# A contiguous table of the earlier vectors, and two constant matmuls per step, in a 64-matrix Householder tridiagonalisation

## What is computed

```
deg = jnp.sum(A, axis=-1)
Lap = deg[..., :, None] * jnp.eye(n, dtype=A.dtype) - A
Lap_norm = d_isqrt[..., :, None] * Lap * d_isqrt[..., None, :]
_, U = jnp.linalg.eigh(Lap_norm)
agg = jnp.einsum('bmn,bmd->bnd', U, features)
```

## Time and profile before

| | |
|---|---|
| median of 3 runs | 5151.7 us |
| lowest, highest | 5149.34, 5155.43 us |
| the profiled execution | 5160.19 us |
| its span, first to last instruction | 5157.9 us |
| mean granted TensorE clock over the span | 0.686 of 2.4 GHz |

### The profile page before, as it was taken

How to read it: one execution, slowest core, us unless ns; L and a number is a source line. 1 busy time by engine, 2 the same in 40 slices (tenths; PEclk the granted TensorE clock), 3 DMA queues, 4 the chain that set the end, 5 groups by cost and what they waited for, 6 DMA issues and landing times.

```text
span 5157.9 us, 57427 instructions
## 1 busy us (share of the span) xinstructions
PE 2378.0 (46%) x15702; PEld 1593.0 (31%) x15702; DVE 4163.5 (81%) x18604; ACT 1313.2 (25%) x4350; POOL 122.0 (2%) x53
## 2 busy tenths in 40 slices
PE   0555555555526717519349063344105821020399
PEld 0222222233324314215124063243105820020266
DVE  4788878888779999999999888686996979989522
ACT  0000000011113233242342233122442412224154
POOL 0000000000000000000000010010003100000000
PEclk9766666665556857758668576676557965555699
DMA  6000000000110000000000112005000030020120
GB/s 144 14 15 25 25 16 19 19 22 25 30 31 9 9 9 17 0 9 17 9 1 0 17 31 45 0 9 124 0 0 9 17 124 0 0 114 0 49 66 17
DMA packets 142060, 140.50 MB, mean 27 GB/s; under 512 B 28445, under 2 KB 128426, under 8 KB 134826
## 3 DMA queue, kind: packets, MB, share of 16 engines
q1 hardware_dynamic: 141738, 136.97, 9.8%
HBM read 110.43 MB, written 26.41 MB: 27 GB/s over the span
## 4 chain that ended last, share of the span: by engine, by line
DVE 60%; PE 27%; DMA 5%; issue 4%; ACT 3%; SPq 1%; DVEq 0%; ACTq 0%; PEldq 0%
PE psum L2038 7%; PE psum L1678 5%; DVE big_a L381 2%; DVE gvec L385 2%; DVE big_b L1107 2%; PE psum L2062 2%; DMA big_b<-rows_dram 1%; DVE vt L529 1%; PE psum L2240 1%; DVE big_b L716 1%; DMA vt<-pairs_dram 1%; DVE sc_t L951 1%; DVE big_b L707 1%; DVE big_b L711 1%; DVE big_a L953 1%
## 5 line engine op out<-in xcount | busy, mean ns | idle before, releaser
L2038 PE MATMUL psum<-big_a 128*32 128x508 f32 (+59 forms) x4032 | 443.7, 606 | 54.1 <-issue 50.9
L1627 PE MATMUL psum<-plane,big_a 128*128 128x128 f32 x192 | 50.2, 430 | 608.8 <-ACT big_a L1543 587.2
L2013 PE MATMUL psum<-plane,big_b 128*128 128x128 f32 x126 | 54.6, 433 | 442.7 <-DVE big_b L396 442.1
L2038 PEld LDWEIGHTS psum<-big_a 128*32 128x32 f32 x4032 | 174.3, 157 | 255.0 <-issue 175.5
L1678 PE MATMUL psum<-big_b 128*128 128x512 f32 x544 | 245.5, 613 | 0.0
L2234 PE MATMUL psum<-plane,big_b 128*128 128x128 f32 x192 | 37.7, 378 | 443.2 <-DVEq L1308 426.7
L2224 PE MATMUL psum<-big_b 128*128 128x128 f32 x384 | 71.7, 372 | 349.7 <-ACT big_b L2138 349.7
L1627 PEld LDWEIGHTS psum<-plane,big_a 128*128 128x128 f32 x192 | 36.0, 220 | 622.6 <-ACT big_a L1543 599.6
L1837 DVE TENSOR_REDUCE f_ln<-psum 128x4 f32<-128x512 f32 x32 | 22.1, 689 | 233.6 <-PE psum L1952 157.8
L1996 ACT COPY big_a<-psum 128x64 f32<-128x64 f32 x109 | 29.1, 267 | 662.7 <-PE psum L2047 662.7
L2219 PE MATMUL psum<-vt,big_b 128*128 128x128 f32 (+1 forms) x384 | 72.3, 375 | 261.1 <-ACT big_b L1330 261.1
(11 more groups left out here) (729 smaller groups left out, 9270.4 us busy)
## 6 DMA issues: line engine op xcount, KB each, us to landing
big_a<-rows_dram SPq DMA_DIRECT2D x4, 4096.0 KB, 13.9
vt<-pairs_dram SPq DMA_DIRECT2D x504, 32.0 KB
big_a<-rows_dram SPq DMA_DIRECT2D x4, 2048.0 KB, 17.3
pairs_dram<-big_a SPq DMA_DIRECT2D x252, 32.0 KB, 1.8
big_a<-rows_dram SPq DMA_DIRECT2D x2, 3072.0 KB, 15.6
big_b<-rows_dram SPq DMA_DIRECT2D x2, 3072.0 KB, 22.5
big_b<-adj SPq DMA_DIRECT2D x2, 2048.0 KB, 17.6
big_b<-adjT SPq DMA_DIRECT2D x2, 2048.0 KB, 39.5
```

The costliest lines, as they stand in the source:

```text
L1627: ins = t.transpose(psum[0:parts, bank, g * N:(g + 1) * N], src(g), ident)
L2013: t.transpose(psum[:, 1, 0:SLOTS], x_rows[0:SLOTS, k % 2, :], whole).then_inc(S("x_node_ps"), 1)
L2038: ins = t.matmul(psum[i * SPAN:i * SPAN + MW, 0, 0:4 * wide], v_masked[:, i, q * MW:(q + 1) * MW], anode[:, g:g + 4, k + 1:N + 2 * u], sta ...
```

## The change

**The table.** `ring` goes. The pairs now lie in `past` (P), an array of 128 x 16 in `big_a`: for one element the values of all the panel's vectors are contiguous, 64 bytes from element to element. Lines 317 and 381 then walk over the vectors first and over the elements second, reading P and writing T in runs of 2u contiguous values.

**Its upkeep.** v and w are still written as contiguous rows, because TensorE and the DMAs read them: v to `v_rows` (8 rows in `big_b`), w to `w_rows` (4 rows of its own, a tile that the kernel before had allocated and not used). Two `tensor_copy` on VectorE per step put them into P as well: the w row in `reflect`, behind the norm of x and before the square root is asked for (u > 0, 109 times), and v in `advance`, between the sum of line 385 and the dot product of line 389 (all but the last step of a panel, 109 times). The stores of w must now have landed four steps back, where before a slot of the ring was reused after eight.

**The constant matmuls.** After the transposition of v, in steps with k < 64, u > 0 and not the last of the panel, TensorE does two fp32 matmuls of the identity with 512 columns of `plane`, a constant. They write PSUM bank 7, which nothing reads before the panel's update overwrites it. These are 45 steps and 90 matmuls.

```diff
-        ring = carve(PAIRS // 2, 2, N)
+        past = carve(N, PAIRS)
-        x_rows = big_b[:, 0:2 * N].rearrange("p (k n) -> p k n", n=N)
+        VR = 8
+        v_rows = big_b[:, 0:VR * N].rearrange("p (k n) -> p k n", n=N)
+        x_rows = big_b[:, VR * N:(VR + 2) * N].rearrange("p (k n) -> p k n", n=N)
...
                 n_x = lp.go(v.tensor_tensor_reduce(junk[:, x], raw[:, x], raw[:, x], 1.0, 0.0, ALU.mult, ALU.add, s2x))
-                if k >= FULL:
-                    v.wait_ge(S("v_stored"), 16 * (stored_before(k) + 1))
+                if j:
+                    v.wait_ge(S("w_row"), k)
+                    n_w = lp.go(v.tensor_copy(P[:, k + 1:, many - 1], w_rows[0:SLOTS, (k - 1) % 4, k + 1:]))
+                if k >= VR:
+                    v.wait_ge(S("v_stored"), 16 * (k - VR + 1))
...
                 if j:
-                    pairs = pairs_of(k, u)
-                    partners = ring_h[:, place(k - u):place(k - u) + u, ::-1, k + 1]
-                    v.wait_ge(S("w_row"), k)
-                    lp.go(v.tensor_tensor(by_pair(T[:, live, 0:many]), pairs, over(partners, w, 3), ALU.mult))
-                    n_b = lp.n
+                    partners = P[:, k + 1, 0:many].rearrange("p (j t) -> p j t", t=2)[:, :, ::-1]
+                    lp.after(n_w)
+                    n_b = lp.go(v.tensor_tensor(by_pair(T[:, live, 0:many]), by_pair(P[:, live, 0:many]), over(partners, w, 1), ALU.mult))
...
-                    weights = coef[:, 0:many].rearrange("p (j t) -> p j t", t=2)
-                    lp.go(v.tensor_tensor(by_pair(T[:, live, 4:4 + many]), pairs_of(k, u), over(weights, w, 3), ALU.mult))
+                    lp.go(v.tensor_tensor(T[:, live, 4:4 + many], P[:, live, 0:many], over(coef[:, 0:many], w, 1), ALU.mult))
...
                 v.wait_ge(S("v_row"), k + 1)
+                if u < size - 1:
+                    lp.go(v.tensor_copy(P[:, k + 1:, many], vk))
...
-                if k >= FULL:
-                    v.wait_ge(S("w_stored"), 16 * (stored_before(k) + 1))
+                if k >= 4:
+                    v.wait_ge(S("w_stored"), (k - 3) * 16)
...
-            by_pair = lambda ap: ap.rearrange("p w (j t) -> p j t w", t=2)
-            pairs_of = lambda k, u: ring_h[:, place(k - u):place(k - u) + u, :, k + 1:]
+            by_pair = lambda ap: ap.rearrange("p w (j t) -> p w j t", t=2)
...
                     if u < size - 1:
                         t.wait_ge(S("v_row"), k + 1)
-                        t.transpose(psum[:, 6, 0:SLOTS], ring[0:SLOTS, place(k), 0, :], whole).then_inc(S("v_node_ps"), 1)
+                        t.transpose(psum[:, 6, 0:SLOTS], v_rows[0:SLOTS, k % VR, :], whole).then_inc(S("v_node_ps"), 1)
+                        if u and k < N // 2:
+                            for _ in range(2):
+                                t.matmul(psum[:, 7, :], whole, plane[:, 0:4, :], start=True, stop=True)
```

More of the change, by code:

```diff
@@ L142, in graph_net @@
         anode = carve(B, AW)
-        carve(AW)
-        ring = carve(PAIRS // 2, 2, N)
+        past = carve(N, PAIRS)
         terms = carve(N, 4 + PAIRS)
         PER = 16 // TILES
+        carve(AW)
         v_masked = carve(TILES, PER * (MW + 8))
@@ L274, in v_tridiagonal @@
             st(v.memset(tri_h[:, :, :], 0.0))
+            st(v.memset(w_rows[:, :, :], 0.0))
             st(v.memset(gs_h[:, 0:1], 1e-30))
@@ L283, in v_tridiagonal @@
             own = pl["own"][0:SLOTS, 0:4]
-            ring_h, T = ring[0:SLOTS], terms[0:SLOTS]
+            V = v_rows[0:SLOTS]
+            P, T = past[0:SLOTS], terms[0:SLOTS]
             d_, e_, tau_ = (tri_h[0:SLOTS, i, :] for i in range(3))
@@ L287, in v_tridiagonal @@
             v.wait_ge(leaves_stored, 32)
-            st(v.memset(ring[:, :, :, :], 0.0))
-            st(v.memset(big_b[:, 0:2 * N], 0.0))
+            st(v.memset(big_b[:, 0:(VR + 2) * N], 0.0))
             v.sem_inc(S("tri_started"), 1)
@@ L298, in reflect @@
                 be, tau = e_[:, k:k + 1], tau_[:, k:k + 1]
-                v_new = ring_h[:, place(k), 0, :]
+                v_new = V[:, k % VR, :]
                 v.wait_ge(S("x_row"), k + 1)
                 n_x = lp.go(v.tensor_tensor_reduce(junk[:, x], raw[:, x], raw[:, x], 1.0, 0.0, ALU.mult, ALU.add, s2x))
-                if k >= FULL:
-                    v.wait_ge(S("v_stored"), 16 * (stored_before(k) + 1))
-                if k == FULL + VR - 2:
+                if j:
[3 more added lines that the diff above has]
+                    v.wait_ge(S("v_stored"), 16 * (k - VR + 1))
+                if k == VR - 2:
                     v.wait_ge(S("lap_stored"), 48)
@@ L353, in reflect, with advance @@
                 return n_e
-            def advance(k, u, n_e):
+            def advance(k, u, size, n_e):
                 j, w, many = u, N - k - 1, 2 * u
@@ L359, in advance @@
                 tau = tau_[:, k:k + 1]
-                vk = ring_h[:, place(k), 0, live]
+                vk = V[:, k % VR, live]
                 if not j:
@@ L398, in advance @@
                 n_d = lp.go(v.tensor_tensor(d_[:, k + 1:k + 2], moved[:, k + 1:k + 2], c2, ALU.add))
-                if k >= FULL:
-                    v.wait_ge(S("w_stored"), 16 * (stored_before(k) + 1))
+                if k >= 4:
+                    v.wait_ge(S("w_stored"), (k - 3) * 16)
                 lp.after(n_s)
-                wn = ring_h[:, place(k), 1, live]
+                wn = w_rows[0:SLOTS, k % 4, live]
                 v.scalar_tensor_tensor(wn, vk, a2, scaled[:, live], ALU.mult, ALU.add).then_inc(S("w_row"), 1)
                 lp.after(n_d)
-            by_pair = lambda ap: ap.rearrange("p w (j t) -> p j t w", t=2)
-            pairs_of = lambda k, u: ring_h[:, place(k - u):place(k - u) + u, :, k + 1:]
+            by_pair = lambda ap: ap.rearrange("p w (j t) -> p w j t", t=2)
             def stale_of(k, u):
@@ L422, in v_tridiagonal @@
                         n_e = reflect(b0 + u, u)
-                    advance(b0 + u, u, n_e)
+                    advance(b0 + u, u, size, n_e)
                     lp.rewind()
@@ L2024, in t_tridiagonal @@
                         t.wait_ge(S("w_row"), k)
-                        t.transpose(psum[:, 5, 0:SLOTS], ring[0:SLOTS, place(k - 1), 1, :], whole).then_inc(S("w_node_ps"), 1)
+                        t.transpose(psum[:, 5, 0:SLOTS], w_rows[0:SLOTS, (k - 1) % 4, :], whole).then_inc(S("w_node_ps"), 1)
                     t.wait_ge(S("x_weights"), k + 1)
@@ L2304, in _ @@
             sy.wait_ge(S("tri_started"), 2)
-            sy.dma_start(pairs_dram[N - 2:, 0].rearrange("k g n -> g k n"), ring[0::2, VR - 2:, 0, :]).then_inc(S("lap_stored"), 16)
+            sy.dma_start(pairs_dram[N - 2:, 0].rearrange("k g n -> g k n"), v_rows[0::2, VR - 2:, :]).then_inc(S("lap_stored"), 16)
             def pair_rows(k, u, c):
@@ L2316, in _ @@
                     sy.wait_ge(S("v_row"), k + 1)
-                    sy.dma_start(pairs_dram[k, 0], ring[0::2, place(k), 0, :]).then_inc(S("v_stored"), 16)
+                    sy.dma_start(pairs_dram[k, 0], v_rows[0::2, k % VR, :]).then_inc(S("v_stored"), 16)
                     if u:
@@ L2320, in _ @@
                     sy.wait_ge(S("w_row"), k + 1)
-                    sy.dma_start(pairs_dram[k, 1], ring[0::2, place(k), 1, :]).then_inc(S("w_stored"), 16)
+                    sy.dma_start(pairs_dram[k, 1], w_rows[0::2, k % 4, :]).then_inc(S("w_stored"), 16)
                     if u == 0 and k_panel:
```

## The result

The changed kernel takes 5069.06 us in the median of 4 runs (5064.97 to 5076.41), the kernel before, beside it, 5150.62 (5149.34 to 5155.43). The ratio is 0.9842, 95% interval [0.9826, 0.9857]: 81.6 us less, where 76 less (5076 us) was predicted and 5040 to 5112 was the range.

A forecast was written before the change was run, and what follows sets the result against it. VectorE was taken to bound `advance` alone and, with TensorE's matvec, the way to line 369. The table's -53.7 us and the clock's -22 made -76 from 5151.7, so 5076 us; range 5040 to 5112.

The forecast's parts named there:

- What bounds: Tridiagonalisation step: up to line 369 the longer of VectorE's `reflect` and TensorE's matvec decides; after it, `advance` is VectorE alone.
- The products: Lines 317 and 381: contiguous runs take them from 2.07 to about 1.06 ns per element, saving 53.2 us each.
- The copies: 109 of w in `reflect`, 109 of v in `advance`: 14.2 us for w, 3.9 for v after free time.
- The second half: `advance`, line 369 to the next x row: -53.2 us from line 381, +3.9 for copying v, -49.3 in sum.
- The table alone: Both halves of the step without the constant matmuls: -49.3 us after line 369, -4.4 before it, -53.7 together.
- The clock: Constant matmuls shorten TensorE's idle time, so matvecs at u = 2 and 3, k < 64, run faster: -22 us.
- No help from the clock: Rival: the constant matmuls don't hold TensorE's clock, only the table's gain is left: 5098 us, chance 0.20.
- clock held everywhere: Rival: matvecs at u = 2 to 7, k < 64, all run at 2.4 GHz, -69.2 us: 5029 us, chance 0.12.
- Half rate: Rival: lines 317 and 381 gain only half, 1.55 ns per element: 5104 us, chance 0.08.
- slow rate: Rival: lines 317 and 381 keep their rate, the 218 added copies only cost, +23 us: 5175 us, chance 0.05.
- Cover: Constant matmuls hide behind `advance` at no cost (bound +5 us); no wait for w stores; panel ends keep their length.

The follow-up runs named there:

- the sized matmuls: Changed kernel with constant matmuls sized to end 0.3 us before the next x row, in all steps with u > 0 except a panel's last: 0.9689 against the kernel before.

## Why the prediction was right, point by point

**What bounds.** Right. The two halves of a step behave as described: what VectorE saves in `advance` shortens the step, what it saves in `reflect` becomes waiting. In the kernel with the table alone `reflect` lost 42.7 us and the way to line 369 at u > 0 only 0.7, even less than the 4.4 that were predicted.

**The products.** The mechanism and the rate were right, 1.04 ns (1.06 taken from line 370 in the earlier trace rows). But the term was mis-sized: I counted durations. The slow product had overlapped its follower by 0.18 us and the fast one only by 0.08, so from start to start each product saves 45 to 48 us, not 53.2 (line 381: 104.8 to 62.5 us, and 5.2 in the next gap).

**The copies.** This step failed. I priced them from line 352 at 18.1 us on VectorE's paths. (The working also has a slip: 0.31 us less an overlap of 0.09 is 0.22 us at w = 102, not 0.17, which would have made the price some 11 us higher.) They run at 0.85 ns per element rather than 1.03, which is a detail; the sum of what changed around the v copy in the trace after is -9.2 us, and around the w copy about +2. The runs name the reason for the first: the copy parts two waits of which the second place had cost 0.12 us. In the earlier trace rows I read the 0.23 us between lines 386 and 389 as the way of the sum's result, of which the copy could use a part, and not as a price of two waits that could go.

**The second half.** -49.3 predicted, -56.8 measured at u > 0 and -1.6 at u = 0. That it came out this near is luck, since the two errors have opposite signs: the products gave 6 us less and the copies 13 more.

**The table alone:** -53.7 predicted, -59 measured (-61.0 in the stage, 3.4 of them where the table changes nothing). The second half gave 8.8 more than predicted, the first 3.7 less.

**The clock.** -22 predicted, 22.6 measured in the stage. The mechanism was right, the agreement of the numbers in part luck: I expected u = 2 and 3 and nothing from u = 4 on; the three gave 6.3, 7.0 and 6.8 us, each about half of the 14 to 17 us that the sized matmuls give there. The length of a matvec wholly at 2.4 GHz was also taken a little short: the formula gives 2.67 us for 400 columns, the trace above has 2.91. The idle stretches were estimated well (1.9 us before u = 3 and 2.3 before u = 4; 1.85 and 2.24 in the trace above), and such a stretch may go either way, as the 12 of 17 had said.

**The rivals.** No help from the clock (5098) and clock held everywhere (5029) were both decided by experiments: with two matmuls neither happened; with four the second very nearly did, and 126 us came off where I had worked out 123. With sized ones it was 160, since there the steps with k of 64 and more take part too. Half rate and slow rate are out by the measured 1.04 ns. The Trainium skill ("VectorE: DVE Perf Modes", section "Mode 1× (REGULAR) — the baseline") has fp32 and odd strides work at one result per cycle, with no price for the stride; this case's traces don't agree: the same product on the same elements took 2.07 ns with single elements written 80 bytes apart and 1.04 with contiguous ones. The Trainium skill's rule of two hits per 16-byte line ("SBUF — State Buffer", section "Door 1: The DMA port swizzle", where it comes to cachelines) fits most of what was measured: the writes at 80 bytes, the sums of four and more terms 512 bytes apart, and no penalty for runs of two values at u = 1. It doesn't give the sum of two terms 512 bytes apart, which kept 1.06 ns.

**Cover.** Right: in the changed kernel, as before it, 5 of 125 x transpositions start more than 0.25 us behind their x row, no wait on `w_stored` was seen, the panel ends kept their length (332.9 to 330.8 us).

## What to carry to other kernels

Read the cost of an instruction from its start to the next one's start, and ask of every gap between two short instructions what stands in it: two waits in a row cost 0.12 us in one place here and 0.05 to 0.09 in three others, and where both had long been fulfilled, spreading them over two instructions was worth 17 us for no work at all. An engine that waits at one clock level and starts the next burst at another can be kept up by constant work, but only if the work reaches close to the next burst: two matmuls per step gave 23 us, the same idea sized to the gap 99. And when one of two parallel paths is shortened, look at the wait at their meeting point before counting the gain.

## What the runs showed of the hardware that was not expected

- On VectorE a second wait before an instruction, on a semaphore that had been reached long ago, took 0.12 us (0.23 to 0.11 us between two starts); added instructions that carried the wait made the kernel faster, even with 103 elements each.
- Writing single fp32 elements 80 bytes apart halves the rate of a two-operand product (2.07 against 1.04 ns per element), whether or not the second operand repeats. Summing four or more terms that lie 512 bytes apart takes 1.67 to 1.76 ns per element instead of 1.04; a sum of two such terms takes 1.06. A one-operand scale (line 352) writes 80 bytes apart at 1.03 and contiguously at 0.46 ns.
- Behind 1.85 us of idle time and an x transposition at the upper clock, a matvec ran its first 3.4 us at a granted clock of 0.50; behind 0.55 us it kept 1.00 throughout (4.58 against 2.91 us for 400 columns).
